# Reordering the opening of a two-layer gated transformer kernel on one core

## The reference

```
x = x + tanh(g_xattn[0]) * diff_attention(ctx, layernorm(x))
      # q = norm(x) @ Wq.T, k = ctx @ Wk.T, v = ctx @ Wv.T; 32 score heads of 8, softmax,
      # pairs of heads subtracted with weight lam, times v (16 heads of 16)
x = x + tanh(g_ffn[0]) * ffn(layernorm(x))      # top 3 of 8 zones, gelu, 1024 wide
x = x + tanh(g_xattn[1]) * attention(layernorm(x), ctx)   # 16 heads of 16
x = x + tanh(g_ffn[1]) * gated(layernorm(x))    # silu(gate) * up, 768 wide
```

## Time and profile before

| what | value |
|---|---|
| median of 3 runs | 670.17 us (669.87 to 670.48) |
| the profiled execution, its own time | 670.22 us |
| its span in the profile | 668.4 us |
| mean granted clock of TensorE | 0.977 |
| PE, DVE, ACT, POOL busy | 605.9, 384.4, 356.3, 147.9 us |

### The profile page before, as it was taken

One profiled execution on the slowest core, in us unless ns is written; L12 is line 12 of the kernel. 1 busy time (PEld: TensorE's weight loads), 2 busy tenths in 40 slices (PEclk: granted clock), 3 DMA queues, 4 the chain that ended last, 5 costly groups with the idle time before them and its releaser, 6 DMA issues.

```text
span 668.4 us, 11546 instructions
## 1 busy us (share of the span) xinstructions
PE 605.9 (91%) x4313; PEld 501.9 (75%) x4313; DVE 384.4 (58%) x813; ACT 356.3 (53%) x615; POOL 147.9 (22%) x218
## 2 busy tenths in 40 slices
PE   2688888897899999999999999999778998999998
PEld 2565565554499899999989888899656776878887
DVE  6668676877753524435545534534586663656654
ACT  4335766676765746546557435535775433443421
POOL 9615355444630000000000000000564210210000
PEclk9879989999999999999999999999989998999999
DMA  7302120212030030300313340020132100000000
GB/s 231 103 27 74 46 55 3 54 47 98 32 126 0 4 124 1 111 17 0 126 25 73 78 145 1 2 96 2 48 96 63 36 2 1 33 1 18 16 33 32
DMA packets 23127, 34.76 MB, mean 52 GB/s; under 512 B 4704, under 2 KB 14048, under 8 KB 23072
## 3 DMA queue, kind: packets, MB, share of 16 engines
q1 hardware_dynamic: 20800, 30.51, 14.8%
q0 software_dynamic: 1984, 3.44, 2.2%
q10 hardware_dynamic: 288, 0.07, 0.0%
HBM read 18.93 MB, written 2.10 MB: 31 GB/s over the span
## 4 chain that ended last, share of the span: by engine, by line
PE 74%; DVE 10%; ACT 5%; issue 3%; POOL 3%; DMA 0%; ACTq 0%; DVEq 0%; POOLq 0%
PE PV L1261 21%; PE SC L1294 21%; PE SC L1261 9%; PE PV L1285 5%; PE AUX L1261 4%; PE SC L1408 3%; PE AUX L1375 3%; DVE NM L1136 3%; PE PV L1294 2%; PE AUX L1294 2%; DVE O L1144 2%; ACT PB L908 2%; ACT XN L853 1%; PE AUX L1333 1%; PE PV L1375 1%
## 5 line engine op out<-in xcount | busy, mean ns | idle before, releaser
L994 DVE TENSOR_TENSOR HL<-HF,HH 128x512 fp32r<-128x512 f32 x96 | 67.2, 700 | 153.5 <-ACT HH L950 153.4
L908 ACT ACTIVATE PB<-SC 77x1024 f32<-77x1024 f32 x96 | 95.4, 1015 | 54.6 <-PE SC L1408 54.3
L1294 PE MATMUL SC<-WBH,HL 128*128 128x256 f32 x384 | 108.7, 283 | 0.0
L1294 PE MATMUL SC<-WBH,HH 128*128 128x256 f32 x384 | 108.6, 283 | 0.0
L1294 PE MATMUL SC<-WBL,HH 128*128 128x256 f32 x384 | 108.6, 283 | 0.0
L950 ACT ACTIVATE HH<-PV 128x512 fp32r<-128x512 f32 x96 | 57.3, 597 | 72.1 <-PE SC L1294 72.1
L945 ACT ACTIVATE HF<-PV 128x512 f32<-128x512 f32 x96 | 57.2, 596 | 54.8 <-PE PV L1261 52.8
L718 POOL TENSOR_TENSOR RSTD<-RSTD,NHALF 128x4 f32<-128x4 f32 x16 | 17.8, 1115 | 290.8 <-DVE RSTD L1068 290.8
L1261 PE MATMUL PV<-XH,WAH 128*128 128x512 f32 x192 | 77.6, 404 | 1.0 <-DVE O L1144 1.0
L1294 PEld LDWEIGHTS SC<-WBL,HH 128*128 128x128 f32 x384 | 72.8, 189 | 3.9
L1294 PEld LDWEIGHTS SC<-WBH,HH 128*128 128x128 f32 x384 | 72.5, 189 | 4.0 <-DVE HL L994 0.3
(11 more groups left out here) (252 smaller groups left out, 1216.0 us busy)
## 6 DMA issues: line engine op xcount, KB each, us to landing
QG<-QH SPq DMA_DIRECT2D x96, 64.0 KB, 2.0
WSA<-in_wa SPq DMA_DIRECT2D x6, 1024.0 KB, 5.0
WSB<-in_wb SPq DMA_DIRECT2D x12, 512.0 KB, 6.4
QG<-QL SPq DMA_DIRECT2D x48, 64.0 KB, 2.0
X<-in_x SPq DMA_DIRECT2D x4, 512.0 KB, 6.3
QG<-QH POOLq DMA_DIRECT2D x32, 64.0 KB, 2.3
out_x<-X SPq DMA_DIRECT2D x8, 256.0 KB, 2.3
QG<-QL POOLq DMA_DIRECT2D x16, 64.0 KB, 2.3
```

The source lines that it names most:

```text
L908: act.activation(probs(n)[0:S, :, :], scores(n)[0:S, :, :], ACT.Exp, scale=SCALE[a]).then_inc(exp_done, 1)
L994: return dve.tensor_tensor(dst, raw, hi.bitcast(F32), ALU.subtract)
L1294: ins = pe.matmul(ps[:, D * (t % 2):D * (t % 2 + 1)], lhs[:, block], rhs, start=first and t == 2 * i and n == 0, stop=last and t == 2 * i ...
```

## The change

- Order: `weights_split` 0 (query weights) stands ahead of `weights_split` 1, and `weights_split` 1 is without the value weights, which become step 3, behind `negpart` 0, with a semaphore `wv_in` of their own.
- Statistics of tile 1 stand ahead of `keys` 0; the groups of keys are split 2, 3, 3 (KEYS), in both layers. `query` and `q_move` are split: half 0, the norm of tile 1, half 1, then `keys` 1 and 2.
- `heads_first` builds KA of groups 0 and 1 right behind `keys` 0; `heads` 0, 0 builds the other six groups, behind `first`.
- `scale` counts `xn_ready` after each of its four instructions, and PE waits block by block in every `turn` of c = 0.
- `q_move`: SP takes r = 0, 2 and POOL r = 1, 3; QH is sent twice as soon as it is written, then QL. The first three copies of each have a semaphore of their own (`first_moved`), for which the first `max` waits.
- Both clears of QG are POOL's, behind the norm of tile 0; the clears of PB are a step `clear` behind `q_move` of half 1. The 13 small loads are issued by SP behind its other loads.

The diff without the semaphores' declarations, the moved list of the small loads, the changed counts of `xn_ready` in POOL's waits and the group ranges of the second layer's keys:

```diff
@@ -52,6 +52,7 @@
 SMALL = 13
 LAG = 2
 MIXED = 2 * HC
+KEYS = ((0, 2), (2, 5), (5, 8))
 PARTS = {"turn": (3, KC), "query": (3, KC), "turn_mix": (2, KC), "project": (2, 2)}
 LOAD = {"attend": 2, "values": 3, "max": 1, "negmax": 2, "turn": 2, "turn_mix": 2, "project": 3}
 ROWS = 96
...
@@ -177,10 +178,11 @@
     def moves(a, j):
         return [("q_move", a, j, c) for c in range(KC)]
 
-    steps = norm(ATT0, 0) + [("weights_split", 1), ("weights_split", 0), ("scale", ATT0, 0), ("turn", ATT0, 0)]
-    steps += keys(0, 0, 1) + [("query", 0, 0)] + moves(0, 0) + norm(ATT0, 1) + keys(0, 1, 3) + [("heads", 0, 0)]
+    steps = norm(ATT0, 0) + [("weights_split", 0), ("weights_split", 1), ("scale", ATT0, 0), ("turn", ATT0, 0)]
+    steps += norm(ATT0, 1)[:TT] + keys(0, 0, 1) + [("heads_first",), ("query", 0, 0, 0), ("q_move", 0, 0, 0)]
+    steps += [("norm", ATT0, 1), ("query", 0, 0, 1), ("q_move", 0, 0, 1), ("clear",)] + keys(0, 1, 3) + [("scale", ATT0, 1)]
     first, second = ([("max", 0, 0, t, 8 * i + 4 * u, 4) for t in range(TT) for u in range(2)] for i in range(2))
-    steps += [("scale", ATT0, 1)] + first + [("negpart", 0), ("turn", ATT0, 1)] + second + [("negpart", 1)]
+    steps += first + [("negpart", 0), ("weights_split", 3), ("heads", 0, 0), ("turn", ATT0, 1)] + second + [("negpart", 1)]
     left = []
     for j in range(J):
         side = {}
...
 
-            eng.wait_ge(q_moved[n % 2][c], 16 * sum(6 if m in BOTH else 12 for m in range(n % 2, n + 1, 2)))
+            eng.wait_ge(q_moved[n % 2][c], 16 * sum((3 if (m, c) == (0, 0) else 6) if m in BOTH else 12
+                                                    for m in range(n % 2, n + 1, 2)))
             if n in BOTH:
-                eng.wait_ge(pool_moved[n][c], 16 * 6)
+                eng.wait_ge(pool_moved[n][c], 16 * (3 if (n, c) == (0, 0) else 6))
+            if (n, c) == (0, 0):
+                for i in range(2):
+                    eng.wait_ge(first_moved[i], 16 * 3)
 
         def ffn_half(i, h):
...
             sp.dma_start(WQR[:, :, :], chunks(wq0)).then_inc(wq0_in, 16)
-            for dst, src in ((CR, ctx_t), (WKR, wk0), (WVR, wv0)):
+            for dst, src in ((CR, ctx_t), (WKR, wk0)):
                 sp.dma_start(dst[:, :, :], chunks(src)).then_inc(kv_in, 16)
+            sp.dma_start(WVR[:, :, :], chunks(wv0)).then_inc(wv_in, 16)
             for j in range(1, J):
                 sp.dma_start(X[:, TT * j:TT * (j + 1), :], x[j]).then_inc(x_in[j], 16)
             sp.dma_start(WQ1R[:, :, :], chunks(wq1)).then_inc(wq1_in, 16)
             sp.dma_start(WOR[:, :, :], chunks(wo)).then_inc(wo_in, 16)
             sp.dma_start(W1[:, :, :], chunks(w1)).then_inc(wo_in, 16)
+            for dst, src in small:
+                sp.dma_start(dst, src).then_inc(small_in, 16)
             for step in PLAN:
                 kind = step[0]
                 if kind == "q_move":
...
-                    for r in range(2 if n in BOTH else 4):
-                        for q, src in enumerate((QH, QL, QH)):
+                    sp.wait_ge(qh_ready, order["query", a, j, c] + 1)
+                    for r in range(0, 4, 2 if n in BOTH else 1):
+                        moved = first_moved[0] if (n, c, r) == (0, 0, 0) else q_moved[n % 2][c]
+                        for q, src in ((0, QH), (2, QH), (1, QL)):
+                            if r == 0 and q == 1:
+                                used(sp, ("query", a, j, c))
                             sp.dma_start(QG[n % 2][32 * q:32 * q + 32, 4 * c + r, :].bitcast(F32),
-                                         src[32 * r:32 * r + 32, c, :].bitcast(F32)).then_inc(q_moved[n % 2][c], 16)
+                                         src[32 * r:32 * r + 32, c, :].bitcast(F32)).then_inc(moved, 16)
                 elif kind == "negmax":
 
                     _, a, j, c = step
...
             pool.wait_ge(pool_set, 7)
-            pool.memset(QG[1][ROWS:P, :, :].bitcast(F32), 0.0).then_inc(qg_set[1], 1)
-            pool.wait_ge(qg_set[1], 1)
             chain = 0
             for step in PLAN:
                 kind = step[0]
...
                 elif kind == "weights_split" and step[1] == 0:
-                    for dst, src in small:
-                        pool.dma_start(dst, src).then_inc(small_in, 16)
                     pool.wait_ge(rstd_ready, 1)
+                    for queries, cleared in zip(QG, qg_set):
+                        pool.memset(queries[ROWS:P, :, :].bitcast(F32), 0.0).then_inc(cleared, 1)
+                    for cleared in qg_set:
+                        pool.wait_ge(cleared, 1)
+                elif kind == "clear":
+                    pool.wait_ge(rstd_ready, 2)
                     for buffer in PB + PB2[0]:
                         pool.memset(buffer[64:P, :, :], 0.0).then_inc(pb_set, 1)
                     pool.wait_ge(pb_set, 4)
...
                     dup_hi(WQ1R)
-                elif kind == "weights_split":
-                    act.wait_ge(kv_in, 48)
+                elif kind == "weights_split" and step[1] == 1:
+                    act.wait_ge(kv_in, 32)
                     act.activation(CH[:, :, :], CR[:, :, :], copy).then_inc(split_hi, 1)
                     dup_hi(WKR)
+                elif kind == "weights_split" and step[1] == 3:
+                    act.wait_ge(wv_in, 16)
                     act.activation(WVH[:, :, :], WVR[:, :, :], copy).then_inc(split_hi, 1)
                 elif kind == "turn":
...
                     for t in range(TT):
-                        ins = act.activation(XN[:, t, :], X[:, TT * j + t, :], ident_f, scale=RSTD[:, 1, t:t + 1],
-                                             bias=RSTD[:, 3, t:t + 1])
-                    ins.then_inc(xn_ready, 1)
+                        act.activation(XN[:, t, :], X[:, TT * j + t, :], ident_f, scale=RSTD[:, 1, t:t + 1],
+                                       bias=RSTD[:, 3, t:t + 1]).then_inc(xn_ready, 1)
                 elif kind == "keys" and step[2] < 3:
                     _, a, i = step
                     key = step + (0,)
-                    groups = range(3 * i, min(3 * i + 3, G))
+                    groups = range(*KEYS[i])
                     filled(act, key)
                     if a == 0:
...
@@ -982,7 +1002,6 @@
         def _(dve):
             chain = [0]
             dve.memset(PV[:, :, :], 0.0).then_inc(pv_set, 1)
-            dve.memset(QG[0][ROWS:P, :, :].bitcast(F32), 0.0).then_inc(qg_set[0], 1)
 
             def link(ins):
...
 
-            def keys_by_head(a, b):
-
-                if b == 0:
+            def keys_by_head(a, b, groups, ready):
+
+                if groups.start == 0 and b == 0:
                     dve.memset(KALL[a][:, B * HEADS[a] * S:B * HEADS[a] * S + WIDE].bitcast(F32), 0.0)
                 for s in range(NS[a]):
-                    dst = KA[a][:, b, :, :].rearrange("p (g s) n -> p g s n", s=NS[a])[:, :, s, :]
+                    dst = KA[a][:, b, :, :].rearrange("p (g s) n -> p g s n", s=NS[a])[:, groups, s, :]
                     col = s + (NS[0] if a else 0)
-                    ins = dve.tensor_scalar(dst, KT[a][:, :, b * S:(b + 1) * S].bitcast(F32),
+                    ins = dve.tensor_scalar(dst, KT[a][:, groups, b * S:(b + 1) * S].bitcast(F32),
                                             pick[:, col:col + 1], None, ALU.mult)
-                ins.then_inc(ka_ready, 1)
+                ins.then_inc(ready, 1)
 
             for step in PLAN:
                 kind = step[0]
                 if kind == "weights_split" and step[1] == 0:
-                    dve.wait_ge(split_hi, 4)
+                    dve.wait_ge(split_hi, 1)
                     lo_part(WQ0L[:, :, :], WQR[:, :, :], WQ0H[:, :, :]).then_inc(split_done, 1)
                 elif kind == "weights_split" and step[1] == 1:
-                    dve.wait_ge(split_hi, 1)
+                    dve.wait_ge(split_hi, 2)
                     lo_part(CL[:, :, :], CR[:, :, :], CH[:, :, :])
-                    dve.wait_ge(split_hi, 2)
-                    dup_lo(WKR)
                     dve.wait_ge(split_hi, 3)
+                    dup_lo(WKR).then_inc(split_done, 1)
+                elif kind == "weights_split" and step[1] == 3:
+                    dve.wait_ge(split_hi, 4)
                     lo_part(WVL[:, :, :], WVR[:, :, :], WVH[:, :, :]).then_inc(split_done, 1)
                 elif kind == "stats":
                     _, stage, j, t = step
...
                         dve.wait_ge(sc_ready, A0_UNITS)
-                    keys_by_head(a, b)
+                    keys_by_head(a, b, slice(2 if (a, b) == (0, 0) else 0, G), ka_ready)
+                elif kind == "heads_first":
+                    used(dve, ("keys", 0, 0, 0))
+                    dve.wait_ge(const_in, 32)
+                    dve.wait_ge(pool_set, 7)
+                    keys_by_head(0, 0, slice(0, 2), ka_first)
                 elif kind == "query":
                     _, a, j, c = step
```

(28 more changed lines are left out.)

36 lines of the change are left out of this document (18 added, 18 removed).

## The result

The changed kernel takes **664.61 us** in the median of six runs (662.23 to 665.28) against 669.73 (669.01 to 670.48) for six of the kernel before on the same chip: a ratio of 0.9912, with an interval of 0.9895 to 0.9928, or 5.1 us less. Forecast were 665.7, in 663.0 to 667.6. The profiled execution took 662.89 us for a span of 661.1, at a mean granted clock of 0.982.

A forecast was written before the change was run, and what follows sets the result against it. TensorE, busy 91% of the span, was taken as the bound, except in the opening, which waits for VectorE. Attention 4.9 us earlier, plus 0.2 and 0.2 lost, made -4.5 and 665.7 us, range 663.0 to 667.6.

The forecast's parts named there:

- the low clock: Around the maxima: the granted clock, 0.52 before the change, was expected to be low again; net effect taken as 0.
- GpSimd's slack: GpSimd's queue of clears, copies and tile 1's norm, from 8.7 us on: about 1 us to spare.
- rival (c): GpSimd's queue becomes late: tile 1's norm ends at 24.5, past the allowed 22.9, all following 1.6 later; 667.3 us, chance 0.10.
- The 0.66 us of the transposes: Opening: with PE waiting block by block, three transposes of about 0.22 us lie under ScalarE's work, saving 0.66 us.
- The deferred work: Moved work is paid between the two sets of reductions: 5.0 us there instead of 3.53.
- the term for disturbance: GpSimd's PB clears beside VectorE's WVL and KA: cost nothing to 1.1 us, taken as 0.2.
- Rival (a): GpSimd's clears collide with VectorE: slower WVL and KA, late copies, 1.3 us beyond the 0.2 allowed; 667.0 us, chance 0.12.
- (e): Slower: 13 small loads stand ahead of the QG copies in the DMA ring, attention near 77; 710 us, chance 0.03.
- the term for the late pace: Query matmuls: if TensorE's quicker pace comes as late as before, 0 to 1.4 us lost, taken as 0.2.
- the later part: Later turns, second-layer key groups and earlier copies behind attention's start: from -1 to +1 us, taken as 0.
- (b): The clock stays up through the maxima: 1.7 us less in attention, 0.5 in negpart and the turn; 663.5 us, chance 0.13.
- (d): No measurable change: the lead is lost in another wait behind attention's start; 668.8 to 671.5 us, chance 0.04.

The follow-up runs named there:

- pool_small: Kernel after the change, with the 13 small loads issued by GpSimd again, ahead of its two QG clears; 670.68 us, ratio 1.0005.
- whole_wait: Kernel after the change, with PE waiting at each turn for all four XN blocks instead of block by block; 663.75 us, ratio 0.9905.
- heads_whole: Kernel after the change, with KA of all eight groups built ahead of the first maximum; 664.10 us, ratio 0.9908.
- after_again: Kernel after the change, repeated and profiled again unchanged; 664.24 us, ratio 0.9905.
- both_warm: Kernel after, value weights split earlier, PB clears behind six-group KA, plus unread key matmuls among the first 16 maxima and behind tile 1's transposes; 661.79 us.
- before_again: Kernel before the change, profiled once more unchanged; 669.50 us.

## Why the prediction was right, and where it was not

**Right in place and size.** The statistics behind X (4.64 for 4.65), the norm (8.88 for 8.69), the query (14.01 for 13.85), the first reduction (21.56 for 21.3), the end of eight (24.74 for 24.6), WVH with VectorE idle beside it (1.33 us in its bracket), and the low clock. pool_small shows the small loads free on SyncE, and vital off GpSimd. GpSimd's slack was real: the norm of tile 1 ends at 21.70, before the 22.9 of rival (c). The 0.66 us of the transposes are real, by whole_wait. The deferred work is a loan, as heads_whole shows.

**Wrong in size: the term for disturbance, 0.2 us, was 1.4.** The step "I take 0.2, since a clear only writes" failed, and so did "nothing to 1.1 us". KA of six groups took 2.96 and 3.06 beside the PB clears, 1.56 without them. Between the two sets of reductions it was 6.0 us (24.73 to 30.75) instead of 5.0, and attention was at 34.13 and 34.70 instead of 32.95. Rival (a) named the mechanism but spread it wrongly: WDL and WVL, with two operands in SBUF, took 1.83 and 0.69 beside clears, as without, and the copies were not late by it: the first maximum did wait for a copy, one of the signs named for (a) or (e), but GpSimd had stood idle for 1.62 us when it sent its first at 17.13. Beside clears only KA is held. The clears of QG end at 15.51, and KA of two groups starts at 15.70: that collision was missed by 0.2 us.

The Trainium skill, GPSIMD Engine Reference, section Key points, names VectorE's two-port modes and its two-input instructions as those in contention with GpSimd. The Trainium skill, VectorE: DVE Perf Modes, section "Mode 2×_2P — use both read ports for one tensor", puts a tensor_scalar on fp32 in SBUF among the first. By KA's rows that part agrees. By WDL and WVL the second part does not hold beside a memset; beside GpSimd products, which read, it does. WOL has WVL's form and two operands in SBUF, and takes 1.48 us instead of 0.69 (kernel after):

```profile
125.17 1.06 POOL L818 TENSOR_TENSOR O<-O,RZ 128x512 f32<-128x512 f32 x1
125.30 1.48 DVE L1013 TENSOR_TENSOR WOL<-WOR,WOH 128x512 fp32r<-128x512 f32 x1
```

**Unsteady: the term for the late pace, 0.2.** From the query's first matmul to QH the kernel before takes 1.76 us, after 1.87 and after_again 2.66: the term was 0.1 in one profile and 0.9 in the other, inside the stated 0 to 1.4, and it moves attention by as much. The premise that the granted clock "stands at 1.00 in 12.62 to 27.34" reads the view too far: the trace's record of the clock begins at 17.48 us in the kernel before, just when the pace of the matmuls doubles, and the view gives 1.00 for the time ahead of it.

**Wrong in size: the later part, 0, was -1 to -2.** From -1 to +1 was allowed. Against the first profile of before, attention is 3.7 and 3.2 us earlier in the two profiles of after, and the spans are 7.3 and 5.0 shorter, so 3.6 and 1.8 us came later. Of that 0.5 to 0.7 us in the second layer are there at equal clock; its keys now go in groups of 2, 3 and 3, so that twelve matmuls instead of 18 stand ahead of the first by-head work, but no run undid that alone, and it is argued only. Another 0.2 is in the last stage, untested too. In the first profile 1.3 and 1.6 more are the clock in other places. That this is all of it in the median is not shown, and pool_small speaks for something lasting: there attention starts 2.2 us later than in the kernel before, and twelve runs take the same time. So the total came right in part by luck, by two errors that cancel: 0.8 to 1.3 us less won at attention (3.2 to 3.7 where the sum had 4.5), and 1 to 2 us more behind it, where the sum had nothing.

**The rivals.** (b) did not come: 0.50 from 26.67 to 34.13. And where the clock was held up on purpose, its 2.7 us did not reach the median, so the 663.5 given for it stood on an assumption (that the rest stays) that both_warm speaks against. (c), (d) and (e) did not come; pool_small is (c) made true, together with (a).

## What to carry to other kernels

When work moves to GpSimd, look at what VectorE runs at that moment, and put clears behind VectorE's one-tensor instructions on SBUF, not beside them: the order alone was worth 1.4 us of VectorE here and 1.2 to 1.8 us at attention, which the time showed only once the value split was moved too. A step moved from ahead of a wait to behind it is only deferred: follow it to where it is paid. Compare stretches at equal granted clock before giving a gain behind the changed part to the change, and ask two profiles, not one. Measure a step as a distance from the event ahead of it: counted from the start of the profile, whole_wait's 0.7 us look like 0.4 (statistics of tile 1 at 13.96 instead of 13.60), since its first XN came earlier by chance.

## What the runs showed of the hardware

- A VectorE tensor_scalar on one SBUF tensor is held by a GpSimd memset for whole instructions: four of 462 elements took 1.56 us alone, 2.96 to 3.28 beside the end of four clears, 4.74 beside all four, 3.85 with these halved; four of 154 took 0.93 alone and 7.49 beside two clears of 3.5. The whole clears hardly suffer: 3.62 alone and 3.88 to 4.13 for four.
- A VectorE tensor_tensor with two operands in SBUF (128x512) took 0.69 us beside such clears and 1.48 beside GpSimd products.
- Matmuls added to keep the clock at 1.00 through 20 to 44 us gave 2.7 us in the stretch behind and none in the median. Why another half-speed stay then came elsewhere remains open.
- A stay of 3.4 us at half speed cost 1.2 to 1.6 us in three stretches, and nothing between the first feed-forward and the last stage: 342.64 us with one (after_again) and 342.64 with none (before_again).
- The first keys and the start of the query ran at the slow pace (0.16 us to the next 154-column matmul at 13 us, 0.09 at 17.2). The trace's record of the clock begins at 14.54 us in the kernel after and at 16.03 in after_again; the granted 1.00 of the views ahead of that is no reading.
